# One-core transformer layer: the second norm's statistics move from VectorE to GpSimd, and three jobs beside the attention steps move

## What is computed

```
x = x + attention(layernorm(x))     # 16 heads of 16, rotary on the last 256 tokens
x = x + experts(layernorm(x))       # 16 experts, each takes its 128 best tokens, and a shared one
layernorm(x) = (x - mean(x)) / sqrt(var(x) + 1e-5)
```

## Time and profile before

| | us |
|---|---|
| median of 3 runs (lowest, highest) | 2324.01 (2321.23, 2324.03) |
| profiled execution, its own time | 2325.04 |
| its span, first to last instruction | 2323.0 |
| batches 1 to 6 of the attention, each | about 169.7 |
| feed_forward, from about | 1460 to 2323 |
| busy over the span: PE, DVE, ACT, POOL | 2180.6, 1861.4, 1561.1, 1054.9 |

### The profile page before, as it was taken

How to read it: one execution, slowest core, us unless ns; L and a number is a source line. 1 busy time by engine, 2 the same in 40 slices (tenths; PEclk the granted TensorE clock), 3 DMA queues, 4 the chain that set the end, 5 groups by cost and what they waited for, 6 DMA issues and landing times. The chain is left out here.

```text
span 2323.0 us, 42151 instructions
## 1 busy us (share of the span) xinstructions
PE 2180.6 (94%) x15502; PEld 1267.5 (55%) x15502; DVE 1861.4 (80%) x3099; ACT 1561.1 (67%) x3060; POOL 1054.9 (45%) x1561
## 2 busy tenths in 40 slices
PE   5899999999999999999999997799999999999996
PEld 3233333333333333333333324688888888888886
DVE  6899999999999999999999993677655555555552
ACT  2598999999999998999999886333333343343341
POOL 3543565465465456456451230000024666666663
PEclk7799999999999999999999998899999999999998
DMA  4002012122122122122112111422324545445442
GB/s 115 8 24 35 17 44 69 35 62 64 37 65 54 35 60 54 35 62 51 35 50 47 33 44 69 143 94 97 98 84 109 112 89 116 108 89 117 111 87 32
DMA packets 204836, 156.20 MB, mean 67 GB/s; under 512 B 110080, under 2 KB 185728, under 8 KB 204672
## 3 DMA queue, kind: packets, MB, share of 16 engines
q1 hardware_dynamic: 180096, 120.47, 18.7%
q0 software_dynamic: 24576, 33.57, 8.6%
HBM read 78.50 MB, written 50.33 MB: 55 GB/s over the span
## 5 line engine op out<-in xcount | busy, mean ns | idle before, releaser
L628 DVE TENSOR_REDUCE sb_MX<-ring 128x1 f32<-128x512 f32 x2048 | 1281.2, 683 | 43.8 <-PE ring L932 20.8
L774 ACT ACTIVATE sb_PR<-rot 128x512 f32<-128x512 f32 x2048 | 1118.7, 611 | 120.2 <-PE rot L943 106.3
L932 PE MATMUL ring<-sb_KT,sb_QT 32*128 32x512 bf16 x2048 | 503.0, 391 | 74.0 <-DVE sb_MX L628 61.0
L954 PE MATMUL pv<-sb_PR,sb_VA 128*32 128x512 f32 x4096 | 547.2, 606 | 2.3 <-ACT sb_OT L828 0.6
L932 PEld LDWEIGHTS ring<-sb_KT,sb_QT 32*128 32x128 bf16 x2048 | 122.1, 91 | 670.4 <-DVE sb_MX L628 612.8
L1286 ACT ACTIVATE ff_GL<-ff_gu 128x512 f32<-128x512 f32 x192 | 114.7, 598 | 514.6 <-PE ff_gu L63 512.2
L943 PE MATMUL rot<-sb_QT,sb_KT 32*128 32x512 bf16 x2048 | 405.5, 386 | 0.9
L61 PE MATMUL ff_gu<-ff_XH,ff_WH 128*128 128x512 f32 x768 | 300.9, 392 | 9.8 <-DVE ff_XL L1339 8.9
L62 PE MATMUL ff_gu<-ff_XL,ff_WH 128*128 128x512 f32 x768 | 300.5, 391 | 0.0
L63 PE MATMUL ff_gu<-ff_XH,ff_WL 128*128 128x512 f32 x768 | 299.9, 391 | 0.0
L1347 DVE TENSOR_TENSOR ff_HF<-ff_GL,ff_gu 128x512 f32<-128x512 f32 x192 | 131.0, 685 | 197.9 <-ACT ff_GL L1286 197.8
(11 more groups left out here) (159 smaller groups left out, 3059.4 us busy)
## 6 DMA issues: line engine op xcount, KB each, us to landing
sb_XA<-x SPq DMA_DIRECT2D x8, 1024.0 KB, 5.5
sb_XR<-x SPq DMA_DIRECT2D x8, 1024.0 KB, 5.8
out<-sb_XR SPq DMA_DIRECT2D x8, 1024.0 KB, 4.5
xn<-sb_XN SPq DMA_DIRECT2D x8, 1024.0 KB, 4.5
xn2T<-sb_XT SPq DMA_DIRECT2D x8, 1024.0 KB, 4.2
ff_XG<-xn2T SPq DMA_DIRECT2D x16, 512.0 KB, 5.4
ff_X<-out SPq DMA_DIRECT2D x16, 512.0 KB, 4.9
ff_W<-WgT SPq DMA_DIRECT2D x16, 512.0 KB, 4.3
```

Source lines behind the costliest of these rows:

```text
L628: nc.vector.reduce_max(MX[:, unit % 2, half, j, qt % 4:qt % 4 + 1], ring[m % RING][:], AX.X).then_inc(ring_done, 1)
L774: out = nc.scalar.activation(PR[V % P_STEPS][:, j, :], R[:], ACT.Exp, scale=0.25)
L932: nc.tensor.matmul(ring[m % RING][:], QT[g][r, P * qt:P * qt + P], KT[g][r, 512 * half:512 * half + 512], start=True, stop=True, tile_posi ...
L954: out = nc.tensor.matmul(pv_bank[head(j), :], VA[b % 2][:, kt, 4 * g + j, :], PR[V % P_STEPS][:, j, :], start=(kt == 0), stop=(kt == TT - 1))
```

## The change

`statistics` gets the argument `n` and now serves both norms: for the second (n = 1) it reads `XR` and writes the centred tokens to `XN2`. It runs in eight steps `MIDDLE`, `inverse_root(1)` in step 34, `normalise` (now with the scaling alone) in 36 to 39, `rope` in step 40 in place of 29. VectorE's four L594 a batch are gone, but for those after the last step. In `BESIDE`, `proj` 6 and 7 go from steps 16, 18 to 14, 15; the four `xt` from 19, 20, 21, 23 to 17, 18, 20, 21; `q` and `k` of tiles 4 and 5 from 40, 43, 44, 45 to 37 to 40; the four `x2t` from 37, 39, 41, 42 to 41, 42, 44, 45.

```
-              16: (-1, "proj", 6), 18: (-1, "proj", 7), 19: (1, "xt", 0, 0),
-              20: (1, "xt", 1, 0), 21: (1, "xt", 0, 1), 23: (1, "xt", 1, 1), 24: (1, "q", 6), 25: (1, "k", 6),
+              14: (-1, "proj", 6), 15: (-1, "proj", 7), 17: (1, "xt", 0, 0),
+              18: (1, "xt", 1, 0), 20: (1, "xt", 0, 1), 21: (1, "xt", 1, 1), 24: (1, "q", 6), 25: (1, "k", 6),
...
-              32: (1, "k", 1), 33: (1, "q", 2), 34: (1, "k", 2), 35: (1, "q", 3), 36: (1, "k", 3), 37: (-1, "x2t", 0, 0),
-              39: (-1, "x2t", 1, 0), 40: (1, "q", 4), 41: (-1, "x2t", 0, 1), 42: (-1, "x2t", 1, 1),
-              43: (1, "k", 4), 44: (1, "q", 5), 45: (1, "k", 5), 47: (-1, "lg", 0), 48: (-1, "lg", 1), 49: (-1, "lg", 2),
+              32: (1, "k", 1), 33: (1, "q", 2), 34: (1, "k", 2), 35: (1, "q", 3), 36: (1, "k", 3), 37: (1, "q", 4), 38: (1, "k", 4), 39: (1, "q", 5),
+              40: (1, "k", 5), 41: (-1, "x2t", 0, 0), 42: (-1, "x2t", 1, 0), 44: (-1, "x2t", 0, 1), 45: (-1, "x2t", 1, 1), 47: (-1, "lg", 0), 48: (-1, "lg", 1), 49: (-1, "lg", 2),
...
+    MIDDLE = (22, 23, 25, 26, 29, 30, 32, 33)
...
+            def statistics(n, b, part):
+
+                src, to = (XA, XA) if n == 0 else (XR, XN2)
...
+                def centre(half):
+                    for quarter in (2 * half, 2 * half + 1):
+                        c = slice(2 * quarter, 2 * quarter + 2)
+                        own.inc(nc.gpsimd.tensor_tensor(to[:, c, :], src[:, c, :],
+                                                        average[:, c].unsqueeze(2).to_broadcast([P, 2, H]), ALU.subtract))
...
+                    else:
+                        pool.wait_ge(x1_ready, TT * (b + 1))
+                        pool.wait_ge(xn2_out, 16 * b)
...
-                if b and S == 27:
-                    inverse_root(1, b)
+                if b and S in MIDDLE:
+                    statistics(1, b - 1, MIDDLE.index(S))
+                if b and S == MIDDLE[-1] + 1:
+                    inverse_root(1)
...
-                if more and S == 29:
+                if b and 36 <= S <= 39:
+                    normalise(1, b, XN2, xn2_ready, S - 36)
+                if more and S == 40:
                     rope(b + 1)
-                if b and 33 <= S <= 36:
-                    normalise(1, b, XN2, XR, xn2_ready, S - 33)
...
-                if prev and 21 <= S <= 24:
-                    if S == 21 and b > 1:
-                        for h in range(2):
-                            dve.wait_ge(xn2_ready[h], 2 * (b - 1))
-                    dve.wait_ge(x1_ready, TT * (b - 1) + 2 * (S - 20))
-                    gather_stats(1, XR, S - 21)
```

More of the change, by code:

```diff
@@ L440, in fold @@
                     own.inc(nc.gpsimd.tensor_tensor(to, s[:, :, 0:width], s[:, :, width:2 * width], ALU.add))
-            def statistics(b, part):
+            def statistics(n, b, part):
+                src, to = (XA, XA) if n == 0 else (XR, XN2)
                 by_tile = sums[:].rearrange("p (t c) -> p t c", t=TT)
                 by_half = sums[:].rearrange("p (t c) -> p t c", c=H)
+                def centre(half):
[3 more added lines that the diff above has]
+                                                        average[:, c].unsqueeze(2).to_broadcast([P, 2, H]), ALU.subtract))
                 half = part // 2 % 2
@@ L448, in statistics @@
                 if part == 0:
-                    pool.wait_ge(rope_done, ROPE_TILES * (2 * max(b, 1) - 1))
-                    pool.wait_ge(xa_in, 16 * (b + 1))
-                    own.inc(nc.gpsimd.tensor_tensor(by_tile, XA[:, :, 0:H // 2], XA[:, :, H // 2:H], ALU.add))
+                    if n == 0:
+                        pool.wait_ge(rope_done, ROPE_TILES * (2 * max(b, 1) - 1))
+                        pool.wait_ge(xa_in, 16 * (b + 1))
+                    else:
+                        pool.wait_ge(x1_ready, TT * (b + 1))
+                        pool.wait_ge(xn2_out, 16 * b)
+                    own.inc(nc.gpsimd.tensor_tensor(by_tile, src[:, :, 0:H // 2], src[:, :, H // 2:H], ALU.add))
                 elif part == 1:
@@ L459, in statistics, with inverse_root @@
                     own.wait(pool)
[L460 to L463, removed]
+                    centre(0)
                 elif part == 4 or part == 6:
                     own.wait(pool)
-                    own.inc(nc.gpsimd.tensor_tensor(by_half, XA[:, i, :], XA[:, i, :], ALU.mult))
+                    own.inc(nc.gpsimd.tensor_tensor(by_half, to[:, i, :], to[:, i, :], ALU.mult))
                     if part == 4:
[L468 to L471, removed]
+                        centre(1)
                 else:
                     fold(by_half, H, 1, deviation[:, i].unsqueeze(2))
-            def inverse_root(n, count):
+            def inverse_root(n):
                 y = rstd[n]
[L478 to L482, removed]
+                own.wait(pool)
+                own.inc(nc.gpsimd.tensor_scalar(spread[:], deviation[:], 1.0 / H, EPS, ALU.mult, ALU.add))
                 own.wait(pool)
@@ L492, in inverse_root, with normalise @@
                 nc.gpsimd.tensor_tensor(y[:], y[:], refine[:], ALU.mult).then_inc(rstd_ready[n], 1)
-            def normalise(n, b, out, src, ready, quarter):
+            def normalise(n, b, out, ready, quarter):
                 pool.wait_ge(rstd_ready[n], b)
@@ L498, in normalise @@
                 shape = [P, 2, H]
[L499 to L502, removed]
                 nc.gpsimd.tensor_tensor(out[:, i, :], out[:, i, :], rstd[n][:, i].unsqueeze(2).to_broadcast(shape),
@@ L558, in _ @@
                 if b == 0 and S in EARLY:
-                    statistics(1, EARLY.index(S))
+                    statistics(0, 1, EARLY.index(S))
                 if b == 0 and S == EARLY[-1] + 1:
-                    inverse_root(0, 1)
+                    inverse_root(0)
                 if b + 2 < B and S in LATE:
-                    statistics(b + 2, LATE.index(S))
+                    statistics(0, b + 2, LATE.index(S))
                 if b + 2 < B and S == LATE[-1] + 1:
-                    inverse_root(0, b + 2)
-                if b and S == 27:
-                    inverse_root(1, b)
+                    inverse_root(0)
+                if b and S in MIDDLE:
+                    statistics(1, b - 1, MIDDLE.index(S))
+                if b and S == MIDDLE[-1] + 1:
+                    inverse_root(1)
                 if more and 13 <= S <= 16:
-                    normalise(0, b + 2, XA, XA, xn_ready, S - 13)
-                if more and S == 29:
+                    normalise(0, b + 2, XA, xn_ready, S - 13)
+                if b and 36 <= S <= 39:
+                    normalise(1, b, XN2, xn2_ready, S - 36)
+                if more and S == 40:
                     rope(b + 1)
-                if b and 33 <= S <= 36:
-                    normalise(1, b, XN2, XR, xn2_ready, S - 33)
                 if b and S == 52:
@@ L750, in _ @@
                 gather_stats(1, XR, pair)
-            dve.wait_ge(stats_ready[1], TT // 2 * B)
+            dve.wait_ge(stats_ready[1], TT // 2)
             for k in range(RSQRT_STEPS):
```

## The result

The changed kernel took 2297.54 us (median of 4 runs, 2295.85 to 2300.4) against 2322.91 (4 runs, 2321.23 to 2324.03): ratio 0.9893 [0.9875, 0.991]. That is 25.4 us faster where 18.4 were forecast, and it lies 4 us under the low end of the range. The profiled run took 2297.27, with a span of 2295.5 (before: 2323.0 of 2325.04).

What follows compares the result with a forecast made beforehand. VectorE was taken to bound the kernel. Batches 1 to 6 (-15.0), batch 7 (-1.9) and batch 0 (-1.5) summed to -18.4 us: 2306.6 profiled, 2305.6 as median, range 2301.5 to 2311.5.

Steps and rivals of the forecast that it cites:

- The bound: Attention steps: VectorE sets the pace, busy 165.8 of a batch's 169.7 us, with ScalarE 14.6 us behind.
- The sum over the steps: Attention steps: -2.5 us in each of batches 1 to 6, -1.9 in batch 7, -1.5 in batch 0, total -18.4.
- The pair at step 19: Steps 17 to 19: a 0.25 us VectorE wait goes, xt beside pv costs up to 0.29; together nothing.
- L594 and q: Steps 19 to 27: four VectorE instructions and tile 6's q wait for xt go, -2.19 us a batch, batches 1 to 6.
- The jobs' other places: Steps 28 to 45: moved q, k and x2t give -0.3 us a batch, bounds 0 and -0.6.
- The joins: VectorE's joins, some waiting for GpSimd instructions: net +0.1 us a batch, bounds -0.1 and +0.7.
- Rival B: Joins of steps 27, 35, 43 wait for GpSimd: 10 us lost at most by the walk, 2312 to 2315; chance 0.12.
- GpSimd fits: Steps 22 to 39: GpSimd's 39 us of work fits in 46, some 3 us slack at step 40, cost nothing.
- rival D: GpSimd late for step 36's split; TensorE waits at step 40, each batch losing what exceeds 3 us slack; chance 0.05.
- After the last step nothing changes: Behind the attention's last step: no change in time, feed_forward only starts earlier; 0 us.
- The range: Whole kernel: 2301.5 to 2311.5 us, from the jobs, the joins and some 1 us for the median.

Runs made afterwards that it cites:

- the filling: 30 matmuls before the last batch's first x2t and 56 transposes at feed_forward's start, results unread, added to the kernel before: 2318.73 us.
- the filled pair: The changed kernel and the kernel before, each with the same unread matmuls and transposes added after the steps: 2301.15 us and 2318.73 us.

## Why the prediction was right or wrong

**The bound: right.** VectorE set the pace and still does. No L594 is left before the last step, and the stretch from step 19 to 27 is 20.41, forecast at about 20.6.

**The sum over the steps: right in its parts, 2 us short.** Batches 1 to 6 gave 2.72 each where 2.5 were forecast, batch 0 gave 1.9 (1.5) and batch 7 gave 2.0 (1.9), 20.2 in all. Term by term: from the batch's start to the join of step 27 it is 2.37 less. The pair at step 19 is -0.25 (the wait that went) and +0.21 (xt beside `pv`), so nothing together, as I had it. L594 and q, forecast at -2.19, then have at most -2.33. Batch 0, which had no L594, shows the difference: its stretch lost 1.61, which is 1.23 for q, 0.24 for the wait at step 20, and 0.14 that I had no term for. The jobs' other places were -0.3 and are -0.36 (-0.47 and +0.11). The joins were +0.1 and are nothing: the join of step 27 does wait, 0.48 and not 0.18, but its stretch is as long as before. The 0.14 and the joins' 0.1 are most of the 0.2 a batch.

**Rival B: the wait is there, the price isn't.** One new wait of 0.30 is hidden, and one old one of 0.67, taken away, gave 0.31. I priced such waits one for one.

**GpSimd fits: right, with less room than I said.** The slack was 2.0 us, not 3, since the split comes 3.9 and not 3.2 us into its step. At 4.7 beyond it the loss per batch is 7.2: rival D's 1 us for 1 us was too cheap, since the wait of 4.38 us was followed by 7 us at a mean granted clock of 0.58. Of D, "each batch loses what exceeds the slack" is refuted.

**"After the last step nothing changes": the step that failed.** The instructions are the same, but their time isn't fixed. The tail was 899.0 before, and 891.8, 898.9 and 896.0 in the three profiles of the changed kernel, with TensorE at the lower level for 37.5, 23.75, 37.75 and 34.25 us of it. I sized the term at 0 and gave it about 1 us of the range; it varied by 7. The profile that was compared caught a short one, and all four runs of the first measurement lie in the lower heap. With the 19.0 to 20.3 us of the steps alone the time would have been 2302.6 to 2303.9, inside the range. Even the steps' part depends on which profiles are compared: the kernel before has its last `pv` group at 1424.05 and, with the filling, at 1423.43. That the short tail is an effect of the change is not shown, nor that it isn't: the short times came in 9 of the changed kernel's 14 runs and seldom in the kernel before. Against an effect of the statistics stand the filled pair, where the kernel before has the shorter tail, and the table of jobs alone, with 894.2. What brings the short tail about stays open.

**The range: not quite the sum of its unknowns.** Added up in 7 batches, they make 2301.1 to 2312.9 (0.3 down or up for the jobs, 0.2 down or 0.6 up for the joins, and 1 us for the median), where I wrote 2301.5 to 2311.5. The measured 2297.54 lies outside both, because of the tail.

## What to carry to other kernels

An engine that paces everything is worth relieving even where its helper needs seven times as long (20.5 us of GpSimd's time for 2.8 of VectorE's here), as long as whoever reads the helper's product is placed behind the time at which the helper has it ready. With the readers in their old places the same edit cost 31 us. When an instruction is taken away, look for the wait it was covering: a batch that lacks the instruction shows it. And when the same tail of identical instructions appears in two profiles, compare its length before trusting a difference of a few us: here it moved by 7 between executions of one kernel.

## What was not expected of the hardware

- TensorE's granted clock fell 16 us after the last `pv` group although the engine was kept busy (16.11 of 16.11 us ahead of the fall), so filling idle stretches with small matmuls (32 rows) did not hold it. Within executions of one kernel it was at the lower level for 23.75 to 37.75 us of the tail. Logits of 32 matmuls took 3.76 or 6.85 us, at the upper and at the lower of its two levels (2.4 and 1.2 GHz).
- A single stall of 4.4 us in the midst of the steps was followed by about 7 us mostly at 1.2 GHz: a `pv` group took 1.94 instead of 1.07 us. The stall then cost 7.2.
- The join, a VectorE maximum of 128x16 with two inputs in SBUF, waited for GpSimd's operations of 128x1024 (0.18 became 0.85) and 128x512 (0.48), but the one of the earlier trace rows with the pow of 128x8 did not wait at all.
